# A lead scale per column in the down projection of a fused cross-attention and mixture-of-experts kernel

## Chip, cores and metric

One core of a Trainium2 chip. The metric is device time in microseconds, the median of three runs; a profiled execution was taken beside them.

## What is computed

```python
x = x + jnp.tanh(g_xattn[0]) * _L0_xattn_ref(ctx_512, _layernorm(x, axis=-1), L0_xattn_W, L0_xattn_b)
x = x + jnp.tanh(g_ffn[0]) * _L0_ffn_ref(_layernorm(x, axis=-1), L0_ffn_gate_w, ...)

# _L0_ffn_ref, for all tokens, with E, K, H, I, GS = (16, 4, 512, 384, 128)
probs = jax.nn.softmax(x @ gate_w.T, axis=-1)
vals, idx = jax.lax.top_k(probs, K)
w = vals / jnp.sum(vals, axis=-1, keepdims=True)
combine = jnp.einsum('tke,tk->te', jax.nn.one_hot(idx, E, dtype=x.dtype), w)
w_gu = dequant_fp4(gate_up_packed, gate_up_scales)
act = swiglu(jnp.einsum('th,ehi->eti', x, w_gu))
w_d = dequant_fp4(down_packed, down_scales)
y_e = jnp.einsum('eti,eih->eth', act, w_d)
out = jnp.einsum('te,eth->th', combine, y_e)
act_s = swiglu(x @ dequant_fp4(shared_gate_up_packed, shared_gate_up_scales))
out = out + act_s @ dequant_fp4(shared_down_packed, shared_down_scales)
```

x is 4 x 512 tokens of 512. Every token goes through one shared expert and four of sixteen routed ones. A weight is a 4-bit code times an fp32 scale, one scale per output column and group of 128 input rows; a routed down matrix has three such groups (`IC` = 3).

## The kernel before

**Products.** fp32 accuracy is had from f16 products: an activation is split into a high and a low f16 half, and so is a scale, so that a weight is the sum of two f16 tiles, code times high scale and code times low scale (`wdn[:, buf, hl]`, and `wgu` likewise). For each group three products are summed in PSUM: high x high, high x low, low x high. The down projection of one tile of 128 tokens is therefore nine products of 128x128 by 128x512 (`down`, L1235).

**Tiles and slots.** The shared expert takes sixteen tiles of 128 tokens. Meanwhile the kernel routes: it sorts tokens by expert into slots of up to 128 tokens, 72 slots in all with these inputs. The experts take 4, 5, 5, 4, 4, 4, 5, 5, 4, 5, 4, 4, 4, 5, 5 and 5 slots. Each engine runs its own program over the slots.

- TensorE (`slot`): first half of gate/up, transposes of the last slot's activation (L1221), transposes of the next slot's rows (L1247), second half of gate/up (L1207), then the down products of the slot before. A down group waits for `yev_done`, the evacuation of y two slots earlier (two PSUM banks, `y_ps`).
- ScalarE: `sg` (silu, L615), the high half of `act` (L622), two copies out of PSUM (L629, L640), and `take_y`, which copies y to SBUF with a constant scale (L646).
- VectorE: `act` (L991), the low half (`low_halves`, L996), and the dequant of the *next* expert's weights. `dequant` has four gate/up parts and four down parts (L897 to L933) and `expert` lays them out by hand, one pair beside each slot: in the first slot after `act` part 0 of down and part 1 of gate/up, in the next two likewise; then the copy of the following expert's words (`take_words`, L945), the last down part beside the fourth slot and the first gate/up part for the expert after. `dqg_ready` (L950) and `dq_ready` (L956) tell TensorE that the weights are there.
- GpSimd: for slot s it gathers the rows of slot s + 4, copies slot s's row numbers (`idx_s`, L520), waits for y (`yev_done`) and issues the scatter that adds y to the output in DRAM (L530).
- SP issues the loads and stores. `load_words` brings an expert's codes, `load_scales` its scale halves, both counted on the semaphore `ld_w[buf]`, for which `take_words` waits: 9 loads an expert, 16 counts each.

**The front.** All scales are loaded as one block and split by five VectorE operations (L709 to L713); SP stores the halves to DRAM, from where `load_scales` spreads them over partitions for each expert. Then come layer norm, the cross-attention mix (`attend`, L755), the dequant of the shared expert, and the first two shared tiles' `act`. Behind the last down part of the shared expert VectorE copies expert 1's words (`take_words(1, 1)`), then adds the mix for batch 1 (`attend(1)`), adds the first y (`add_y`, L1000) and takes the statistics of batch 1.

**Order.** Every engine's order is the order of the code; nothing reorders. A wait holds all behind it on its engine.

## Time and profile before

| | |
|---|---|
| median of 3 runs | 688.45 us (687.16 to 690.41) |
| the profiled execution | 687.41 us, its span 685.6 us, mean granted TensorE clock 0.982 of 2.4 GHz |
| busy in the span | PE 629.7 us (92%), DVE 488.1 (71%), ACT 325.3 (47%), POOL 326.2 (48%) |
| instructions | 17258; L1207 x2112 and L1235 x792 on TensorE |
| DMA | 93.72 MB, mean 137 GB/s |

PE is TensorE, DVE VectorE, ACT ScalarE, POOL GpSimd, SPq the queue of SP. "Busy" is a mean over stages: up to about 180 us the shared expert and the routing run, from 184 to 675 us the routed slots. The time of one execution is its span and 1.8 us around it.

### The profile page before, as it was taken

Reading aid. Unit: us, or ns where it says so; the run is one execution under the profiler, and the core shown is the slowest. Engines: PE = TensorE matmul, PEld = TensorE weight load, DVE = VectorE, ACT = ScalarE, POOL = GpSimd, SP = SyncE. Lnnn points to the kernel's source line nnn. Section 1 sums busy time; section 2 is a strip of 40 time slices with the busy share of each in tenths; the row PEclk is TensorE's granted clock in tenths of the full one; section 3 lists DMA queues with packets and bytes.
Section 4 is the critical chain, followed back from the end, with each engine's and each line's share of the span. In section 5 each row is a group of like instructions: output and inputs, shape, how many; then the busy total and the mean of one; then the engine's idle time right before and its main releaser. Section 6 shows DMA issues by size and latency. Waiting matters only on the chain.

```text
span 685.6 us, 17258 instructions
## 1 busy us (share of the span) xinstructions
PE 629.7 (92%) x4394; PEld 382.1 (56%) x4395; DVE 488.1 (71%) x1271; ACT 325.3 (47%) x558; POOL 326.2 (48%) x506
## 2 busy tenths in 40 slices
PE   3768969999998999999999999999999999999992
PEld 2444536557554656565665656566565656656561
DVE  6979779895766858588888767778588878767110
ACT  1763567331343455454544554454554545455541
POOL 3621834100334465564646555464655656565432
PEclk9999989999999999999999999999999999999997
DMA  8780101128157875768587594847767587654533
GB/s 234 202 247 2 63 31 64 62 54 276 49 172 160 189 173 127 176 123 195 110 203 176 126 223 74 226 85 201 168 135 183 117 199 158 152 86 77 93 39 39
DMA packets 49841, 93.72 MB, mean 137 GB/s; under 512 B 8840, under 2 KB 16776, under 8 KB 49816
## 3 DMA queue, kind: packets, MB, share of 16 engines
q0 software_dynamic: 16128, 38.35, 30.3%
q1 hardware_dynamic: 32936, 55.04, 27.5%
q8 instruction: 11, 0.18, 0.1%
q10 hardware_dynamic: 752, 0.04, 0.1%
q14 instruction: 14, 0.11, 0.0%
HBM read 65.16 MB, written 28.24 MB: 136 GB/s over the span
## 4 chain that ended last, share of the span: by engine, by line
PE 80%; DVE 6%; DMA 3%; ACT 3%; POOL 3%; issue 2%; SPq 1%; DVEq 0%; POOLq 0%; ACTq 0%
PE gu_ps L1207 45%; PE bank L1235 22%; PE bank L1247 4%; PE bank L1221 4%; DMA dn_sc<-dn_scale_halves 2%; PE bank L1262 1%; DMA room_a<-in_ctx 1%; PE gu_ps L1167 1%; POOL room_a L462 1%; PE bank L1164 1%; PE bank L1191 1%; DVE stats L725 1%; POOL X L445 1%; DVE X L1000 1%; ACT mix_room L581 1%
## 5 line engine op out<-in xcount | busy, mean ns | idle before, releaser
L1207 PE MATMUL gu_ps<-wgu,mix_room 128*128 x1728 | 305.9, 327 | 2.7 <-DVE tick L950 1.6
L1207 PEld LDWEIGHTS gu_ps<-wgu,mix_room 128*128 128x128 f16 x1728 | 166.5, 98 | 114.7 <-issue 7.5
L1235 PE MATMUL bank<-wdn,aT 128*128 (+1 forms) x792 | 186.2, 380 | 3.2 <-ACT aT L629 2.6
L530 POOL DMA_INDIRECT out<-mix_room,idx_s x72 | 122.9, 1707 | 32.4 <-issue 30.9
L629 ACT ACTIVATE aT<-bank 128x768 f16<-128x768 f16 x88 | 71.2, 809 | 139.5 <-PE bank L1221 136.2
L1235 PEld LDWEIGHTS bank<-wdn,aT 128*128 128x128 f16 x792 | 77.6, 98 | 88.8 <-issue 3.6
L501 POOL TENSOR_TENSOR pool_tick<-ones 128x1 f32<-128x1 f32 x144 | 35.7, 248 | 163.6 <-DMA out<-mix_room,idx_s 84.0
L991 DVE SCALAR_TENSOR_TENSOR act<-gu_ps,wslot,sg x72 | 44.5, 618 | 96.4 <-ACT sg L615 84.8
L622 ACT ACTIVATE acth<-act 128x384 f16<-128x384 f32 x88 | 46.0, 523 | 120.1 <-DVE act L991 120.1
L512 POOL DMA_INDIRECT room_b<-token_rows,idx_g x72 | 76.0, 1055 | 12.3 <-issue 3.6
L927 DVE TENSOR_TENSOR wgu<-dq_code,gu_sc 128x768 f16<-128x768 f16 x136 | 72.5, 574 | 2.3
L640 ACT ACTIVATE mix_room<-bank 128x1024 f16<-128x1024 f16 x72 | 73.1, 1015 | 0.0
L1207 PE MATMUL gu_ps<-wgu,xT 128*128 128x384 f16 x384 | 72.7, 344 | 0.0
L615 ACT ACTIVATE sg<-gu_ps 128x384 f32<-128x384 f32 x88 | 43.1, 490 | 61.0 <-PE gu_ps L1207 61.0
L509 POOL COPY idx_g<-room_b 128x1 int32 (+1 forms) x72 | 39.3, 546 | 67.8 <-DVE tick L861 47.2
L996 DVE TENSOR_TENSOR acth<-act,acth (+1 forms) x88 | 49.2, 559 | 29.7 <-ACT acth L622 29.3
L1207 PEld LDWEIGHTS gu_ps<-wgu,xT 128*128 128x128 f16 x384 | 37.8, 102 | 26.2 <-issue 6.0
L1221 PE MATMUL bank<-id,acth 128*128 128x128 f16 x528 | 43.8, 219 | 8.1 <-ACT acth L622 6.0
L1221 PEld LDWEIGHTS bank<-id,acth 128*128 128x128 f16 x528 | 36.1, 98 | 21.8 <-ACT acth L622 10.0
L1247 PE MATMUL bank<-id,room_b 128*128 128x128 f16 x576 | 44.2, 220 | 0.0
L933 DVE TENSOR_TENSOR wdn<-dn_code,dn_sc 128x384 f16<-128x384 f16 x136 | 43.4, 360 | 0.7
L646 ACT ACTIVATE mix_room<-bank 128x512 f32<-128x512 f32 x72 | 41.7, 579 | 3.0 <-PE bank L1235 3.0
(157 smaller groups left out, 588.1 us busy)
## 6 DMA issues: line engine op xcount, KB each, us to landing
dn_sc<-dn_scale_halves SPq DMA_DIRECT2D x34, 384.0 KB
dn_raw<-in_L_ffn_down_packed SPq DMA_DIRECT2D x48, 256.0 KB
gu_sc<-gu_scale_halves SPq DMA_DIRECT2D x34, 192.0 KB
X<-in_x SPq DMA_DIRECT2D x4, 1024.0 KB, 8.4
token_rows<-room_a SPq DMA_DIRECT2D x16, 256.0 KB, 2.2
out<-X SPq DMA_DIRECT2D x4, 1024.0 KB, 11.1
gu_raw<-in_L_ffn_gate_up_packed SPq DMA_DIRECT2D x16, 192.0 KB
gu_raw<-in_L_ffn_gate_up_packed SPq DMA_DIRECT2D x16, 191.9 KB
```

Source lines behind the costliest of these rows:

```text
L512: nc.gpsimd.indirect_dma_start(xg[:, b, :], None, rows_dram[:, :], bass.IndirectOffsetOnAxis(idx_g[:, b:b + 1], 0)).then_inc(xg_ld[b], 16)
L530: nc.gpsimd.indirect_dma_start(out[:, :], bass.IndirectOffsetOnAxis(idx_s[:, b:b + 1], 0), y_sb[:, b, :], None, compute_op=ALU.add).then_i ...
L622: nc.scalar.activation(acth[:, b, 0, :], act[:, b, :], ACT.Copy).then_inc(ah_done, 1)
L629: nc.scalar.activation(aT[:, b].rearrange("p a c t -> p (a c t)"), at_ps, ACT.Copy).then_inc(aT_done, 1)
L640: nc.scalar.activation(xTs[:, b, :], xT_ps, ACT.Copy).then_inc(xTs_done, 1)
L927: link(nc.vector.tensor_tensor(wgu[:, buf, hl, c, :], dq_code[:, :], gu_sc[:, buf, hl, :], ALU.mult), wait=False)
L991: nc.vector.scalar_tensor_tensor(act[:, b, :], gu_ps[:, 2 + b, 0:I], weight, sg[:, b, :], ALU.mult, ALU.mult).then_inc(act_done, 1)
L996: nc.vector.tensor_tensor(acth[:, b, 1, :], act[:, b, :], acth[:, b, 0, :], ALU.subtract).then_inc(al_done, 1)
L1207: mm = nc.tensor.matmul(ps[b][:, 0:I], x(xp * HC + c), wgu[:, w, wp, c, col:col + I], start=(c == 0 and xp == 0 and wp == 0), stop=(c == H ...
L1221: mm = nc.tensor.transpose(at_ps[:, k * P:(k + 1) * P], acth[:, b, hl, t * P:(t + 1) * P], id16[:, :])
L1235: mm = nc.tensor.matmul(y_ps[0 if shared else b][:, :], aT[:, b, ap, t, :], wdn[:, w, wp, t, :], start=(n == 0), stop=(n == 3 * IC - 1))
L1247: mm = nc.tensor.transpose(xT_ps[:, k * P:(k + 1) * P], chunk_h(halves[:, k // HC, :], k % HC), id16[:, :])
```

## The change

The down scales of a routed expert are divided by a *lead* scale per column: that of the first group, so that the first group's scale becomes 1 (where a column's first scale is zero or far smaller than the others, the largest power of two of the others takes its part). A scale of 1 has no low half, so the product high x low of the first group falls away: eight down products per slot. The lead is multiplied back onto y: VectorE takes y out of PSUM times the lead row (`scale_y`), where ScalarE copied it. The shared expert keeps its nine products.

For that
- the routed down scales are loaded apart (`ld_dn`, `dn_all`), the leads found by `lead_exponents` (ahead of the shared dequant) and `lead_scales` (behind its second down part), which also splits the divided scales into halves;
- SP stores those halves and the leads to DRAM when `dn_split` comes, among the stores of token rows, and only then loads expert 1's scales;
- the lead row of each expert is loaded to all partitions (`load_lead`), those of experts 1 and 2 behind the output stores and waited for in `expert(0)` behind `add_y`, the others with the expert's loads;
- `dequant` leaves out the low half of the first group;
- in an expert of five slots or more, the slots from the fourth on all run ahead of the last down part.

```diff
             for b in range(1, B):
                 load_ctx(b)
             load_x(1)
+            for t in range(IC):
+                sp.dma_start(dn_all[:, t, :], dn_scales[:, t, :].rearrange("e (b n) -> e b n", n=HB)).then_inc(ld_dn, 16)
...
             load_words(sp, gu_packed[0], dn_packed[0], 1)
-            sp.wait_ge(st_sc, 64)
-            load_scales(sp, 1, 1)
             for i in range(NT):
+                if i == TB:
+                    sp.wait_ge(dn_split, 1)
+                    for hl in range(2):
+                        for t in range(hl, IC):
+                            sp.dma_start(dn_s_dram[hl, 1:, t, :].rearrange("e (b n) -> e b n", n=HB),
+                                         dn_h[:, hl, t, :]).then_inc(st_dn, 16)
+                    sp.dma_start(lead_dram.rearrange("e (b n) -> (e b) n", n=HB), lead_s[:, :]).then_inc(st_dn, 16)
+                    sp.wait_ge(st_sc, 32)
+                    sp.wait_ge(st_dn, 16 * (2 * IC - 1 + 1))
+                    load_scales(sp, 1, 1)
...
+            for n in (1, 2):
+                load_lead(sp, n, ld_lead)
             sp.wait_ge(dq_ready, 2)
             load_expert(sp, gu_packed[2], dn_packed[2], 1, 3)
+            load_lead(sp, 3, ld_w[1])
...
-            def take_y(r, b):
-                a.wait_ge(y_done, NT + r + 1)
-                if not isinstance(r, int) or r >= 2:
-                    a.wait_ge(added[b], 8 * (r - b))
-                nc.scalar.activation(y_sb[:, b, :], y_ps[b][:, :], ACT.Copy, scale=1.0 / W_SCALE).then_inc(yev_done, 1)
...
                     for hl in range(2):
-                        link(nc.vector.tensor_tensor(wdn[:, buf, hl].rearrange("p t n -> p (t n)")[:, cols],
-                                                     dn_code[:, 0:COLS],
-                                                     dn_sc[:, buf, hl].rearrange("p t n -> p (t n)")[:, cols], ALU.mult),
+                        skip = 0 if hl == 0 or shared else max(0, H - d * COLS)
+                        if skip >= COLS:
+                            continue
+                        part = slice(d * COLS + skip, (d + 1) * COLS)
+                        link(nc.vector.tensor_tensor(wdn[:, buf, hl].rearrange("p t n -> p (t n)")[:, part],
+                                                     dn_code[:, skip:COLS],
+                                                     dn_sc[:, buf, hl].rearrange("p t n -> p (t n)")[:, part], ALU.mult),
...
+                    if d == 1:
+                        lead_scales()
                     activations(d // 2, d // 2, shared_w[:, 0:1])
...
+            def scale_y(r, n):
+                v.wait_ge(y_done, r + NT + 1)
+                v.wait_ge(idx_s_ready, r + 1)
+                nc.vector.tensor_tensor(y_sb[:, r % 2, :], y_pair[:, r % 2, :],
+                                        lead_y[:, bass.ds(n - 1, 1), :].rearrange("p k n -> p (k n)"), ALU.mult).then_inc(yev_done, 1)
...
             def routed_slot(r, e):
                 head(r, e)
                 low_halves(r + NT, r % 2)
+                scale_y(r - 1, e + 1)
...
                 if add_last:
                     add_y(NT - 1)
+                    v.wait_ge(ld_lead, 32)
+                else:
+                    scale_y(first - 1, e)
                 for k in range(1, PARTS - 1):
                     with v.If(tiles > k):
                         head(first + k, e)
                         dequant(n, buf_next, k + 1, k, fill=lambda: low_halves(first + k + NT, (first + k) % 2))
+                        scale_y(first + k - 1, e + 1)
                     with v.Else():
                         dequant(n, buf_next, k + 1, k)
                 end_gate_up(n, buf_next)
                 with v.If(tiles > PARTS - 1):
-                    routed_slot(first + PARTS - 1, e)
+                    with v.Fori(PARTS - 1, tiles) as k:
+                        routed_slot(first + k, e)
                 dequant(n, buf_next, None, PARTS - 1)
                 end_dequant(n)
-                with v.If(tiles > PARTS):
-                    with v.Fori(PARTS, tiles) as k:
-                        routed_slot(first + k, e)
...
+                terms = [(t, ap, wp) for t in range(IC) for ap, wp in ((0, 0), (0, 1), (1, 0))
+                         if shared or t or not wp]
```

The order of SP's queue in the front, before: expert 1's words, its scales right behind, then the sixteen stores of token rows (L379).

```order
L309 DMA gu_raw<-in_L_ffn_gate_up_packed 64x1535
L312 DMA dn_raw<-in_L_ffn_down_packed 128x1x512 x3
L318 DMA gu_sc<-gu_scale_halves 128x1x768 [waits st_sc]
L318 DMA gu_sc<-gu_scale_halves 128x1x768
L321 DMA dn_sc<-dn_scale_halves 128x1536 x2
L379 DMA token_rows<-room_a 128x512 [waits xl_ready,xh_ready] x16
```

The same stretch of SP's queue now:

```order
L336 DMA dn_raw<-in_L_ffn_down_packed 128x1x512 x3
L416 DMA token_rows<-room_a 128x512 [waits xl_ready,xh_ready] x4
L408 DMA dn_scale_halves<-wgu 16x8x64 [waits dn_split]
L408 DMA dn_scale_halves<-wgu 16x8x64 x4
L410 DMA dn_lead_scales<-lead_s 128x64
L342 DMA gu_sc<-gu_scale_halves 128x1x768 [waits st_dn,st_sc]
L342 DMA gu_sc<-gu_scale_halves 128x1x768
L346 DMA dn_sc<-dn_scale_halves 128x1536
L346 DMA dn_sc<-dn_scale_halves 128x1024
L416 DMA token_rows<-room_a 128x512 [waits xl_ready,xh_ready] x12
```

The four loads of scales moved behind four row stores, six new stores and a wait for `dn_split`.

VectorE in the third slot of a routed expert, before, from the unpacking of the codes to the copy of the next words:

```order
L916 TENSOR_SCALAR dn_bits<-dn_bits 128x384
L919 TENSOR_SCALAR dq_code<-dq_mag 128x768 [waits dequant_step]
L922 TENSOR_SCALAR dn_code<-dn_bits 128x384
L927 TENSOR_TENSOR wgu<-dq_code,gu_sc 128x768 [waits dequant_step]
L927 TENSOR_TENSOR wgu<-dq_code,gu_sc 128x768
L933 TENSOR_TENSOR wdn<-dn_code,dn_sc 128x384 x2
L1121 UNCONDITIONAL_BRANCH
```

And the same place now, with the branch around it:

```order
L985 TENSOR_SCALAR dn_bits<-dn_bits 128x384
L988 TENSOR_SCALAR dq_code<-dq_mag 128x768 [waits dequant_step]
L991 TENSOR_SCALAR dn_code<-dn_bits 128x384
L996 TENSOR_TENSOR wgu<-dq_code,gu_sc 128x768 [waits dequant_step]
L996 TENSOR_TENSOR wgu<-dq_code,gu_sc 128x768
L1006 TENSOR_TENSOR wdn<-dn_code,dn_sc 128x384 x2
L1175 REGISTER_ALU
L1177 ISA [waits idx_s_ready,y_done]
L1177 REGISTER_ALU
L1177 TENSOR_TENSOR mix_room<-y_pair,xT 128x512
L1210 UNCONDITIONAL_BRANCH
```

The multiply of the last slot's y (`mix_room` holds `y_sb`, `xT` the lead rows) stands behind the dequant part, with a wait for GpSimd (`idx_s_ready`) and TensorE (`y_done`). In the fourth slot it stands right behind the low half (L1070):

```order
L1065 SCALAR_TENSOR_TENSOR act<-gu_ps,wslot,sg 128x384
L1070 ISA [waits ah_done]
L1070 TENSOR_TENSOR acth<-act,acth 128x384
L1175 REGISTER_ALU
L1177 ISA [waits idx_s_ready,y_done]
L1177 ISA
L1177 TENSOR_TENSOR mix_room<-y_pair,xT 128x512
L1218 REGISTER_ALU
L1218 COMPARE_AND_BRANCH
```

Before, the low half was followed there by the branch and the last down part; the multiply is new between them.

## Rows read from the trace of the kernel before

**Rows 1.** The page, part 4: the chain that ended last, by engine.
```profile
PE 80%; DVE 6%; DMA 3%; ACT 3%; POOL 3%; issue 2%; SPq 1%; DVEq 0%; POOLq 0%; ACTq 0%
```

**Rows 2.** The chain in order of time, one routed slot: start us, us, what.
```profile
413.20 1.95 PE gu_ps L1207 x12
415.15 1.94 PE bank L1235 x9
...
419.83 1.30 PE gu_ps L1207 x8
```

**Rows 3.** VectorE's timeline, one expert: start us, us, instruction, [idle before <-releaser].
```profile
309.24 0.62 DVE L991 SCALAR_TENSOR_TENSOR act<-gu_ps,wslot,sg  x1 [0.20 <-issue]
310.59 0.56 DVE L996 TENSOR_TENSOR acth<-act,acth  x1 [0.74 <-ACT acth L622]
...
316.89 0.62 DVE L991 SCALAR_TENSOR_TENSOR act<-gu_ps,wslot,sg  x1 [1.01 <-issue]
...
321.86 0.67 DVE L933 TENSOR_TENSOR wdn<-dn_code,dn_sc 128x384 f16<-128x384 f16 x2
322.84 0.62 DVE L991 SCALAR_TENSOR_TENSOR act<-gu_ps,wslot,sg  x1 [0.31 <-issue]
...
329.55 0.62 DVE L991 SCALAR_TENSOR_TENSOR act<-gu_ps,wslot,sg  x1 [1.34 <-ACT sg L615]
...
336.12 0.62 DVE L991 SCALAR_TENSOR_TENSOR act<-gu_ps,wslot,sg  x1 [0.30 <-issue]
```

**Rows 4.** VectorE's timeline in the front.
```profile
28.63 0.56 DVE L945 COPY gu_half<-gu_raw 128x768 uint16<-128x768 uint16 x1 [1.04 <-DMA dn_sc<-dn_scale_halves]
...
50.78 0.62 DVE L991 SCALAR_TENSOR_TENSOR act<-gu_ps,shared_w,sg 128x384 f32<-128x384 f32 x1 [3.48 <-ACT sg L615]
```

**Rows 5.** The chain in order of time, in the front.
```profile
57.84 0.08 DVE gu_half L945
...
58.31 2.73 DVE X L755 x4
```

**Rows 6.** VectorE's timeline while routing: small operations.
```profile
144.34 0.20 DVE L817 CAST pos_slot<-pos_i 128x64 f16<-128x64 int32 x1
...
147.37 0.42 DVE L791 TENSOR_REDUCE r_sum<-r_exp 128x16 f32<-128x256 f32 x1
```

**Rows 7.** SP's timeline in the front, and by tile the landing of the scale stores.
```profile
18.46 1.25 SPq L318 DMA_DIRECT2D gu_sc<-gu_scale_halves  x2
...
DMA to landing us min/median/max: 4.0/5.0/6.0
```

**Rows 8.** Timelines of VectorE and GpSimd, first routed expert.
```profile
196.18 0.62 DVE L991 SCALAR_TENSOR_TENSOR act<-gu_ps,wslot,sg  x1 [0.62 <-ACT sg L615]
...
201.48 0.18 POOL L520 COPY idx_s<-room_b 128x1 int32<-128x1 int32 x1 [5.59 <-DMA out<-X]
...
214.45 0.57 DVE L945 COPY gu_half<-gu_raw 128x768 uint16<-128x768 uint16 x1 [4.15 <-DMA dn_sc<-dn_scale_halves]
```

**Rows 9.** VectorE's timeline: first `act` of the second and of the last routed expert.
```profile
222.79 0.62 DVE L991 SCALAR_TENSOR_TENSOR act<-gu_ps,wslot,sg  x1 [0.96 <-ACT sg L615]
...
642.90 0.62 DVE L991 SCALAR_TENSOR_TENSOR act<-gu_ps,wslot,sg  x1 [4.65 <-ACT sg L615]
```

**Rows 10.** VectorE's timeline: the add of y to X and the instruction behind it.
```profile
60.96 0.68 DVE L1000 SCALAR_TENSOR_TENSOR X<-bank,X 128x512 f32<-128x512 f32 x1
61.56 0.68 DVE L725 BATCH_NORM_STATS2 stats<-X 128x6 f32<-128x512 f32 x1
```

**Rows 11.** Timelines of ScalarE and GpSimd: y evacuated, scatter, next index copy.
```profile
397.48 0.58 ACT L646 ACTIVATE mix_room<-bank 128x512 f32<-128x512 f32 x1
...
398.90 1.61 POOL L530 DMA_INDIRECT out<-mix_room,idx_s  x1 [0.50 <-issue]
...
413.36 1.61 POOL L530 DMA_INDIRECT out<-mix_room,idx_s  x1 [0.15 <-issue]
...
416.64 0.19 POOL L520 COPY idx_s<-room_b 128x1 int32 x1
```

More of the change, by code:

```diff
@@ L213, in gated_xattn_moe @@
         gu_ps = psum("gu_ps", [P, 4, 512], F32)
-        bank = [gu_ps[:, i, :] for i in range(4)] + [psum(f"bank{i}", [P, 512], F32)[:, :] for i in range(4, 8)]
+        bank4 = psum("bank4", [P, 512], F32)
+        y_pair = psum("y_pair", [P, 2, 512], F32)
+        bank7 = psum("bank7", [P, 512], F32)
+        bank = [gu_ps[:, i, :] for i in range(4)] + [bank4[:, :], y_pair[:, 0, :], y_pair[:, 1, :], bank7[:, :]]
         g_ps, u_ps = bank[0:2], bank[2:4]
@@ L719, in _, with lead_exponents @@
                                          ALU.logical_shift_left), wait=False)
+            s0, s1, s2 = (dn_all[:, t, :] for t in range(IC))
+            e_rest, e_lead, reach, keep, up, own, other, inv = (lead_room[:, k, :] for k in range(8))
+            def lead_exponents():
+                EXPONENT, TINY, DEEP = 0x7F800000, 2.0 ** -100, 2.0 ** -20
+                v.wait_ge(ld_dn, 16 * IC)
+                step(nc.vector.tensor_scalar(e_rest.bitcast(I32), s1.bitcast(I32), EXPONENT, None, ALU.bitwise_and), wait=False)
+                step(nc.vector.tensor_scalar(up.bitcast(I32), s2.bitcast(I32), EXPONENT, None, ALU.bitwise_and), wait=False)
+                step(nc.vector.tensor_scalar(e_lead.bitcast(I32), s0.bitcast(I32), EXPONENT, None, ALU.bitwise_and))
+                step(nc.vector.scalar_tensor_tensor(e_rest, e_rest, TINY, up, ALU.max, ALU.max))
+                step(nc.vector.scalar_tensor_tensor(keep, e_rest, DEEP, e_lead, ALU.mult, ALU.is_le), wait=False)
+                step(nc.vector.scalar_tensor_tensor(reach, e_rest, DEEP, e_lead, ALU.mult, ALU.max))
@@ L867, in _ @@
             G_STEPS, D_STEPS = 6, 5
[L868 removed]
+            N_STEPS = PARTS * (G_STEPS + D_STEPS)
             def end_of(n):
[L872 removed]
+                return (n + 1) * N_STEPS + (1 if isinstance(n, int) and n == E else 2)
             def dequant(n, buf, g, d, fill=None, free=None):
[L878 removed]
+                shared = isinstance(n, int) and n == 0
+                if shared:
                     done = 1 + g * G_STEPS if d is None else 1 + PARTS * G_STEPS + d * D_STEPS
                 elif d is None:
[L881 removed]
+                    done = n * N_STEPS + 2
                 elif g is None:
@@ L979, in _ @@
             row_scores(3)
+            lead_exponents()
             take_words(0, 0)
@@ L1109, in expert @@
                 if buf_next is None:
-                    routed_slot(first, e)
+                    head(first, e)
+                    low_halves(first + NT, first % 2)
+                    scale_y(first - 1, e)
                     with v.If(tiles > 1):
```

83 lines of the change are left out of this document (59 added, 24 removed).

## The prediction

> **What bounds the kernel now.** I read the chain that ended last first. TensorE holds 80% of it and VectorE 6% [rows 1]. In order of time, one routed slot is two gate/up halves of 1.95 us, some transposes, and nine down products in 1.94 us; it comes round every 6.63 us [rows 2]. So TensorE sets the pace, and one product out of nine is 0.216 us. Seventy-two slots make 15.6 us, if nothing else is close.
>
> Something is close. I went through VectorE's timeline over one expert with four slots [rows 3], because VectorE dequantizes the next expert's weights during this expert's slots and must be done by their end. The starts of its `act` instruction lie 7.65, 5.95, 6.71 and 6.57 us apart. Where the idle time before `act` is put down to ScalarE's `sg`, VectorE waited for data; where it says "issue", VectorE itself was late. Only the third distance holds such a wait (1.34 us), so VectorE's own time there is 5.37 us. Its four slots take 7.65 + 5.95 + 5.37 + 6.57 = 25.5 us, TensorE's 4 x 6.63 = 26.5 us. VectorE has 1.0 us to spare in an expert of four slots, and there are eight such experts; the other eight have five.
>
> In the front the chain runs through VectorE itself: the copy of expert 1's words (L945) at 57.84, then `attend`, the statistics and GpSimd [rows 4, 5]. A wait there is on the path one for one.
>
> **The change, part by part.** The sum is made on the profiled execution, 687.4 us, which is 1.0 us under the median of the runs; I add that at the end.
>
> *Scales in the front.* Today expert 1's scales are stored and loaded before VectorE needs them. Now they exist only after `lead_scales`, 15 dependent operations put behind the second down part of the shared expert. VectorE idles there from 47.30 (50.78 less 3.48) [rows 4]. A 64-wide operation took 0.20 us, a 256-wide one 0.42, some 0.04 between them [rows 6]; nine of the first and six of the second kind at 192 wide, some 0.35, are 4.2 us (bounds 3.0 and 6.9). Of these 3.5 lie in the idle time. The halves are ready at 51.5. SP then issues six stores, by the two issues in its row at some 0.6 us each, and a store of scales lands 4.0 to 6.0 us after its issue, median 5.0 [rows 7]; the sixth, issued 3 us after the first, is there at about 59. Only then do the four loads of scales start. For the shared expert the same four were issued from 18.46 and VectorE was released at 28.63 [rows 4, 7], 10.2 us; I take 10, since the queue is emptier and one load a third smaller. That is 69, against 57.84. VectorE's program waits for all loads of that buffer in front of `attend`, so add_y, the statistics and all that follow stand still: **+11 us** (bounds 7 and 15.5: 3.0, 2.5, 4.0 and 8 us, or 6.9, 3, 6.0 and 10.2, counted from 47.3). SP has nothing else to do then; the next row stores wait for the same chain.
>
> The six operations of `lead_exponents` lie where VectorE waits for shared scales anyway (1.04 us before 28.63 [rows 4]); nothing. If they push the start by a microsecond, TensorE's first gate/up, which the chain puts behind transposes, still hides it. The first split is narrower; nothing.
>
> *First expert.* VectorE now waits for the lead rows of experts 1 and 2 behind its last `add_y`. SP issues them behind the last output tile. GpSimd saw that tile landed at 201.48, after 5.59 us of waiting [rows 8]; half that many bytes more take some 2 us, so 203.4. VectorE's `act` of the second slot was at 196.18. Its three remaining slots of this expert, at the costs below (6.1, 7.2, 9.4), end at 226.1 if nothing holds them, 226.8 with a little of TensorE's delay, where the next expert began at 222.79 [rows 9]. The 4.15 us it waited at 214.45 for the next weights [rows 8] vanish, since it comes later itself. **+4 us** (bounds 1 and 6).
>
> *Fourteen experts with a dequant beside them.* Before, from 222.79 to 642.90, 420.1 us [rows 9]. TensorE alone would now need 6.63 - 0.216 = 6.41 a slot: 25.7 and 32.1 us for four and five slots, 404.6 in all. VectorE gets one multiply per slot, 512 wide from PSUM and SBUF. The nearest row is the add to X of the same shape out of the same bank: 0.68 us long, the next instruction starting 0.60 after it [rows 10]. I take 0.62, with its register work hidden behind the running operation. It loses the low half of the first group's down part (half of 0.67 [rows 3]) and a third of a multiply in the second. The Trainium skill ("VectorE: DVE Perf Modes", the section on the TRN2 errata) gives (N+151)/0.96, 691 ns, for an fp32 tensor_tensor; by it the sum would be about 4 us higher. The trace, in which the next instruction starts before the record ends, decides.
>
> A second cost is a new handshake. The multiply waits until GpSimd has copied that slot's index, which lies behind the scatter of the slot before. From ScalarE's copy (ended 398.06) to the scatter's issue it took 0.84 us, from an issue (413.36) to the end of the next index copy 3.47 [rows 11]; together 4.3. In the first three slots VectorE comes to its multiply after the dequant part, about 6 us after the last. In the fourth it comes right behind `low_halves`, about 2.9 us after: 1.0 for the copy of words and 1.9 from `act` to the end of the low halves [rows 3]. So it waits 1.4 us. Four slots then cost 5.95 + 0.62 - 0.33 - 0.1 = 6.1; 5.37 + 0.2 + 0.62 - 0.1 = 6.1; 6.57 + 0.62 = 7.2; 7.4 + 0.62 + 1.4 = 9.4 (7.65 has the loop's back edge, which every second expert has, so 7.4): 28.8 us, over TensorE's 25.7. In five slots the fourth has no dequant: 1.9 + 1.4 + 0.62 + 0.3 = 4.2; the last 7.4 + 0.62 + 1.0 = 9.0. That is 32.6, plus some 1.0 in which VectorE stands waiting for TensorE in the short slot: 33.6. Seven of each are 436.8 us: **+16.7**, the 15.6 us of products already taken out.
>
> Bounds. Below: a multiply of 0.5 and no wait for GpSimd, 26.9 and 32.2 us, 414 in all, -6. Above: 0.25 us of register work per slot and waits of 2.2, 30.6 and 36, 466 in all, +46. ScalarE loses a copy of 0.58 us per slot [rows 11]; it waits elsewhere, so nothing. The extra lead load of each expert comes three slots before it is needed; nothing.
>
> *The last expert* has no dequant: five slots at TensorE's pace, **-1 us**; in the tail VectorE takes y in place of ScalarE, nothing.
>
> Sum: 687.4 + 11 + 4 + 16.7 - 1 = 718.1; on the runs' scale **719 us**.
>
> **Rivals.**
> - *VectorE keeps up.* TensorE still bounds the slots; the fourteen experts fall to 404.6 us (-15.5), the first expert costs +1, the front +11: 684 us, faster. For it: VectorE is far from full on the average over all slots. Against it: the four-slot sum of 25.5 us has no room for four multiplies; it decides when the sum stays under 25.7. With the front hidden as well it would be 674. Chance 0.08 for the two.
> - *The multiply is cheap.* At a third of ScalarE's 0.58 us it is 0.2; the sums fall to 27.1 and 32.6, 418 in all (-2), first expert +3: 699 us. The add to X speaks against it [rows 10]. The Trainium skill ("ScalarE: Activation LUTs", Rules for kernel authors) sends multiplies to VectorE, as up to three times faster in bf16; this one reads fp32 from PSUM. Chance 0.07.
> - *The front is hidden.* If the scales land before VectorE asks, or other work fills the wait: +1 for +11, 709 us. Against it: copy and `attend` are neighbours on the chain [rows 5]. Chance 0.08.
> - *The handshake rules.* Waits for GpSimd or register work in most slots, experts of 30 and 35 us, 455 in all (+35), front and first expert as above: 738 us. Chance 0.15.
>
> **How the numbers follow.** The forecast has 0.62 and by itself runs from 708 to 729. A measurement tells 0.5% from no change, 3.4 us, so same is 685.0 to 691.9. The first rival is mostly under that: faster 0.07; the edges of the first two give same 0.05; slower 0.88. Leaving out the fast end and the upper tail of the handshake, the range is 697 to 741.
>
> **What would show it.** Right: VectorE idle some 10 us before the copy of expert 1's words, released by a load of scales; some 7 us behind the last add_y, released by a lead row; TensorE waiting for ScalarE's or VectorE's act in each expert, most in its last slot; nine products gone to eight at 1.73 us; VectorE over 90% busy from the second expert to the fourteenth. Wrong: slots evenly 6.4 us apart, `act` still behind `sg` everywhere, or the copy of words at its old time.

## The result, and the profile after

The changed kernel takes 758.1 us in the median of four runs (754.04 to 760.26) against 688.7: a ratio of 1.10, interval 1.0947 to 1.1054. The forecast was 719, its range 697 to 741; the sign was right, and the loss is twice and more what was forecast. The profiled execution has a span of 755.9 us, 70.3 more than before.

The page of the changed kernel, busy time by engine, and the chain that ended last:

```profile
PE 636.9 (84%) x4322; PEld 381.0 (50%) x4323; DVE 524.3 (69%) x1314; ACT 290.2 (38%) x486; POOL 332.7 (44%) x506
...
PE 32%; DVE 24%; issue 15%; DMA 10%; POOL 8%; DVEq 5%; ACT 4%; SPq 1%; POOLq 1%; ACTq 0%
```

TensorE's share of the chain falls from 80% [rows 1] to 32%. Its busy time is 7.2 us longer than before, though 72 products of 0.216 us are gone. VectorE, which was to be the bound, is busy 69% of the span, no more than before (71%). So no engine is full; the engines stand waiting for each other. The forecast had given "VectorE over 90% busy from the second expert to the fourteenth" as a sign of being right; it is 72% from 225 to 450 us (162.31 of 225, in the stretches below).

VectorE's timeline at the ends of the stages: the copy of expert 1's words, then the first `act` of the first routed expert, the second `act`, and the first `act` of the second and of the last expert.

```profile
67.78 0.56 DVE L1018 COPY gu_half<-gu_raw 128x768 uint16<-128x768 uint16 x1 [6.57 <-DMA dn_sc<-dn_scale_halves]
...
198.91 0.62 DVE L1065 SCALAR_TENSOR_TENSOR act<-gu_ps,wslot,sg  x1 [0.90 <-ACT sg L658]
...
214.12 0.62 DVE L1065 SCALAR_TENSOR_TENSOR act<-gu_ps,wslot,sg  x1 [9.50 <-DMA xT<-dn_lead_scales]
...
239.36 0.62 DVE L1065 SCALAR_TENSOR_TENSOR act<-gu_ps,wslot,sg  x1 [0.86 <-issue]
...
714.38 0.62 DVE L1065 SCALAR_TENSOR_TENSOR act<-gu_ps,wslot,sg  x1 [1.31 <-issue]
```

Against [rows 4, 8, 9] and the first routed `act` of before (189.59 us), the stages give:

| step | forecast | measured |
|---|---|---|
| front, to the first routed `act` | +11 | +9.3 |
| first expert | +4 | 40.4 for 33.2: +7.2 |
| fourteen experts | +16.7 | 475.0 for 420.1: +54.9 |
| last expert and tail | -1 | 41.5 for 42.7: -1.2 |

So 38 of the 39.6 us that the sum is short of lie in one step. There an expert takes 31.4 us with four slots and 36.5 with five (forecast 28.8 and 33.6; before 27.1 and 32.9). From VectorE's timeline, the last slots of an expert of four, then (from 344.12) the first slot of the next:

```profile
332.30 0.69 DVE L1177 TENSOR_TENSOR mix_room<-y_pair,xT  x1 [0.50 <-POOL idx_s L563]
...
333.87 0.62 DVE L1065 SCALAR_TENSOR_TENSOR act<-gu_ps,wslot,sg  x1 [0.39 <-issue]
335.23 0.56 DVE L1070 TENSOR_TENSOR acth<-act,acth  x1 [0.74 <-ACT acth L665]
337.87 0.69 DVE L1177 TENSOR_TENSOR mix_room<-y_pair,xT  x1 [2.09 <-POOL idx_s L563]
338.48 0.41 DVE L979 TENSOR_SCALAR dn_bits<-dn_raw,dn_shift 128x384 int32<-128x384 int32 x1
...
344.12 0.62 DVE L1065 SCALAR_TENSOR_TENSOR act<-gu_ps,wslot,sg  x1 [0.97 <-issue]
...
352.68 0.62 DVE L1065 SCALAR_TENSOR_TENSOR act<-gu_ps,wslot,sg  x1 [2.84 <-ACT sg L658]
```

and TensorE's in the same time:

```profile
340.34 2.11 PE L1295 MATMUL gu_ps<-wgu,mix_room 128*128 x12
346.15 0.80 PE L1309 MATMUL bank<-id,acth 128*128 128x128 f16 x6 [3.69 <-ACT acth L665]
346.74 1.06 PE L1336 MATMUL bank<-id,room_b 128*128 128x128 f16 x8
347.59 4.05 PE L1295 MATMUL gu_ps<-wgu,mix_room 128*128 x12
```

and GpSimd's, the scatter of the slot before, the next gather with its index, and the index for which VectorE waits:

```profile
333.83 1.61 POOL L573 DMA_INDIRECT out<-mix_room,idx_s  x1 [0.30 <-issue]
334.89 0.92 POOL L552 COPY idx_g<-room_b 128x1 int32 x1
335.90 0.19 POOL L544 TENSOR_TENSOR pool_tick<-ones 128x1 f32<-128x1 f32 x1
336.23 1.02 POOL L555 DMA_INDIRECT room_b<-token_rows,idx_g  x1
337.26 0.19 POOL L563 COPY idx_s<-room_b 128x1 int32 x1
```

In the expert's last slot (act at 333.87) VectorE waits 2.09 us for the index, multiplies, and has the last down part and the next gate/up part still to do: the next `act` comes 10.25 us later. TensorE stands still 3.69 us for it. Then it runs slower: the same twelve products take 4.05 us that took 2.11 before the stop. So the `act` behind comes another 8.56 us later, and now it is VectorE that waits (2.84 us for ScalarE's `sg`, which waits for TensorE). Both kinds of wait in the groups of waits, from 239.4 to 714.4 us, that is, over the fourteen experts (us in total, times, longest):

```profile
DVE mix_room L1177 <- POOL idx_s L563: 46.8, 24, 3.2
DVE act L1065 <- ACT sg L658: 37.7, 28, 2.9
...
PE bank L1309 <- ACT acth L665: 47.6, 14, 4.7
```

The stretches view of the changed kernel (stretch, its length, busy time and count of PE, PEld, DVE, ACT and POOL, then the granted clock of TensorE, DMA share and GB/s):

```profile
225.00:450.00 225.00, 201.17 (x1364) 119.56 (x1362) 162.31 (x396) 84.31 (x148) 114.32 (x175) 0.95 0.66 144
...
346.00:352.00 6.00, 5.85 (x29) 3.58 (x30) 3.73 (x10) 2.20 (x4) 1.51 (x3) 0.53 1.05 258
352.00:358.00 6.00, 6.00 (x46) 3.74 (x45) 5.01 (x14) 2.52 (x5) 1.91 (x5) 1.00 0.66 159
```

and of the kernel before:

```profile
223.00:440.00 217.00, 216.25 (x1537) 130.59 (x1536) 161.76 (x402) 108.15 (x196) 122.21 (x194) 1.00 0.72 163
```

The clock falls from 1.00 to 0.95 over the experts; in the six microseconds behind the stop it is 0.53 of 2.4 GHz, near its lower level of 1.2 GHz, and 1.00 again after.

Not every stop is followed by this. Behind ten of the fourteen (2.71 to 4.67 us long) the twelve products take 3.26 to 4.05 us; behind the other four (2.70 to 3.08 us) they take 2.11, as here:

```profile
315.50 0.49 PE L1309 MATMUL bank<-id,acth 128*128 128x128 f16 x6 [2.95 <-ACT acth L665]
...
316.28 2.11 PE L1295 MATMUL gu_ps<-wgu,mix_room 128*128 x12
```

The ranges overlap, so the length of a stop alone does not decide it. The three experts of four slots begun at full pace took 30.6, 31.3 and 31.1 us, the four begun with slow products 32.2, 31.1, 31.0 and 32.4: the clock makes some 0.7 us of the 2.6 by which such an expert exceeds the forecast.

### The profile page after: what moved, and what is told of

It is laid out like the page before. It is cut to its first block, busy times and chain, and to the rows that moved or that the text cites. A ratio compares the mean times of both kernels' runs of the same rounds, so it can differ in the third digit from the quotient of the medians.

```text
span 755.9 us, 17257 instructions
## 1 busy us (share of the span) xinstructions
PE 636.9 (84%) x4322; PEld 381.0 (50%) x4323; DVE 524.3 (69%) x1314; ACT 290.2 (38%) x486; POOL 332.7 (44%) x506
## 3 DMA queue, kind: packets, MB, share of 16 engines
q0 software_dynamic: 16128, 38.35, 28.8%
## 4 chain that ended last, share of the span: by engine, by line
PE 32%; DVE 24%; issue 15%; DMA 10%; POOL 8%; DVEq 5%; ACT 4%; SPq 1%; POOLq 1%; ACTq 0%
PE gu_ps L1295 19%; PE y_pair L1324 7%; DMA out<-mix_room,idx_s 4%; DVE act L1065 3%; DVE wgu L996 2%; POOL room_b L555 2%; DMA dn_sc<-dn_scale_halves 2%; PE bank L1309 2%; ACT acth L665 2%; DVE mix_room L1177 2%; DVE dn_bits L979 2%; PE bank L1336 2%; DVE wdn L1006 2%; DVE dn_code L991 2%; DVE dn_bits L985 2%
## 5 line engine op out<-in xcount | busy, mean ns | idle before, releaser
L1295 PE MATMUL gu_ps<-wgu,mix_room 128*128 x1728 | 322.6, 339 | 4.3 <-DVE tick L1023 3.4
L1295 PEld LDWEIGHTS gu_ps<-wgu,mix_room 128*128 128x128 f16 x1728 | 171.8, 101 | 126.0 <-issue 26.2
L1324 PE MATMUL y_pair<-wdn,aT 128*128 (+1 forms) x720 | 174.4, 387 | 9.1 <-DVE X L1074 4.5
L544 POOL TENSOR_TENSOR pool_tick<-ones 128x1 f32<-128x1 f32 x144 | 38.2, 266 | 224.4 <-DVE mix_room L1177 157.7
L573 POOL DMA_INDIRECT out<-mix_room,idx_s x72 | 119.1, 1654 | 31.7 <-issue 31.4
L1324 PEld LDWEIGHTS y_pair<-wdn,aT 128*128 128x128 f16 x720 | 71.6, 100 | 90.4 <-issue 14.7
L552 POOL COPY idx_g<-room_b 128x1 int32 (+1 forms) x72 | 61.3, 851 | 64.0 <-DVE tick L929 46.6
L1177 DVE TENSOR_TENSOR mix_room<-y_pair,xT (+1 forms) x72 | 49.5, 688 | 52.5 <-POOL idx_s L563 49.0
L555 POOL DMA_INDIRECT room_b<-token_rows,idx_g x72 | 80.0, 1111 | 10.8 <-issue 0.9
L1070 DVE TENSOR_TENSOR acth<-act,acth (+1 forms) x88 | 49.2, 559 | 29.7 <-ACT acth L665 29.6
L1295 PEld LDWEIGHTS gu_ps<-wgu,xT 128*128 128x128 f16 x384 | 38.5, 104 | 32.7 <-issue 13.2
L982 DVE TENSOR_TENSOR dq_mag<-dq_mag,dq_sign 128x768 uint16<-128x768 uint16 x68 | 39.0, 573 | 2.3
```

Source lines behind the costliest of these rows:

```text
L552: nc.gpsimd.tensor_copy(idx_g[:, b:b + 1], tok[:, bass.ds(s, 1)]).then_inc(idx_g_ready, 1)
L555: nc.gpsimd.indirect_dma_start(xg[:, b, :], None, rows_dram[:, :], bass.IndirectOffsetOnAxis(idx_g[:, b:b + 1], 0)).then_inc(xg_ld[b], 16)
L573: nc.gpsimd.indirect_dma_start(out[:, :], bass.IndirectOffsetOnAxis(idx_s[:, b:b + 1], 0), y_sb[:, b, :], None, compute_op=ALU.add).then_i ...
L1177: nc.vector.tensor_tensor(y_sb[:, r % 2, :], y_pair[:, r % 2, :], lead_y[:, bass.ds(n - 1, 1), :].rearrange("p k n -> p (k n)"), ALU.mult) ...
L1295: mm = nc.tensor.matmul(ps[b][:, 0:I], x(xp * HC + c), wgu[:, w, wp, c, col:col + I], start=(c == 0 and xp == 0 and wp == 0), stop=(c == H ...
L1324: mm = nc.tensor.matmul(y_ps[0 if shared else b][:, :], aT[:, b, ap, t, :], wdn[:, w, wp, t, :], start=(n == 0), stop=(n == len(terms) - 1))
```

## The experiments

**Theory** after the result: the wait for the index and the multiply make VectorE late once in each expert; TensorE stops, and the stop is not made up. **Rivals**: VectorE's work as such is the bound; the order of the loops is; the waits in the front and for the leads return elsewhere.

**1. The index a slot ahead** (GpSimd).

```diff
-                    pool.wait_ge(added[b], 8 * (s - b))
-                nc.gpsimd.tensor_copy(idx_s[:, b:b + 1], tok[:, bass.ds(s, 1)]).then_inc(idx_s_ready, 1)
...
+                    pool.wait_ge(added[1 - b], 8 * (s + b))
+                nc.gpsimd.tensor_copy(idx_s[:, 1 - b:2 - b], tok[:, bass.ds(s if last else s + 1, 1)]).then_inc(idx_s_ready, 1)
                 pool.wait_ge(yev_done, s + 1)
```

> The changed kernel, but GpSimd copies the row numbers of slot s+1 before it waits for y of slot s (as soon as the scatter of slot s-1 has landed), so that the multiply no longer stands behind a scatter and a gather. In the changed kernel VectorE lost 49.0 us to that index in 25 waits of about 2 us, mostly in the last slot of an expert, where TensorE then stood still for 3.7 to 4.7 us and its first gate/up half after the stop took 3.1 to 4.1 us in place of 1.95. Theory 'handshake': the waits go, the last slot's distance falls from 10.2 to about 8.1 us, TensorE's stop is halved and part of the clock comes back: 14 experts times 2 to 3 us, so 715 to 730 us. Rival 'VectorE's work': the multiply and the parts of the dequant that the last slot now carries set the pace, and the wait only fills what would be lost anyway: at most 8 us less, 750 or more.

725.3 us, 1.054 (1.0507 to 1.0581): 32.8 us less, as the handshake theory had it. The fourteen experts fall to 444.0 us, the granted clock from 225 to 660 us is 0.99. From the waits of this run from 240 to 680 us, VectorE's, TensorE's and GpSimd's:

```profile
DVE mix_room L1174 <- POOL idx_s L566: 2.6, 4, 0.9
...
PE bank L1333 <- DMA room_b<-token_rows,idx_g: 13.7, 14, 2.0
...
POOL pool_tick L565 <- DMA out<-mix_room,idx_s: 140.6, 63, 6.2
```

VectorE's wait is gone, and others stand in its place: GpSimd waits longer for the scatter before (140.6 us; in the changed kernel 56.9 from 225 to 680), and TensorE for rows gathered too late.

**2. ScalarE copies y, twice tried.** `scale_y` and its calls are taken out of VectorE's program, `take_y` is put back into ScalarE's; the lead scale is left out of the result.

> The changed kernel, but ScalarE copies y out of PSUM with the constant scale, as before, and VectorE neither multiplies nor waits for the index; the lead scale per column is left out of the result. Eight products, the front, the lead loads and the new order of the loops stay. Theory 'all of it is VectorE's multiply and its wait': the fourteen experts fall from 475.0 us to TensorE's pace, 404.6 to 412, and the total is 687 to 696 us (the front's +9.3 and the first expert's +7.3 remain). Rival 'the order of the loops': the last down part and the first gate/up part in the last slot stop TensorE also without the multiply; then the fourteen experts stay above 430 and the total above 712.

747.8 us, 1.087 (1.084 to 1.0891). By the total that is the rival's, but not by the slots: four experts of five slots took 32.1 to 32.7 us, near TensorE's pace, beside others with one slot of 11 to 13 us. TensorE's waits from 240 to 680 us and the packets of instructions (page, part 3) of this run:

```profile
PE bank L1305 <- issue: 46.1, 12, 10.0
...
q14 instruction: 39, 0.32, 0.2%
```

Shorter code had moved VectorE's loop. So the run was repeated with padding ahead of it:

```diff
-        LEAD = 30
+        LEAD = 68
```

> The run in which ScalarE copies y again, with 68 memsets in place of 30 at the head of VectorE's program, so that VectorE's loop over pairs of experts lies again where it lay in the kernel before (instructions 688 to 987, there 688 to 1013). In the run with 30 VectorE and TensorE stood still up to 10 us at the loop's head for nothing that the trace names but 'issue', and 39 packets of instructions were loaded where the changed kernel loads 15. The lead scale is left out of the result again. Theory 'code loading hid the answer, and VectorE's multiply with its wait is the whole loss': the stops at the loop's head go, packets of instructions fall back to 14 or 15, the fourteen experts take 405 to 415 us and the total is 688 to 698. Rival 'the order of the loops': the experts of four slots stay above 29 us without any stop at the loop's head, total above 705.

694.1 us, 1.0075 (1.0049 to 1.01), 14 such packets, and the fourteen experts at 416.7 us (27.0 and 32.5). The same kernel, 38 memsets longer, is 53.6 us faster. So VectorE's multiply with its wait is worth 475.0 - 416.7 = 58.3 us in the experts, more than the 54.9 that they lost. The order of the loops by itself costs little: experts of five slots, the only ones whose order changed, take 32.5 us here and 31.9 in the old order with the same eight products (experiment 3). (To put back the old order with the multiply in place was not tried: VectorE's loop would grow, and the code's place would speak into the result again. What the order does to the multiply's wait stays open.)

**3. Eight products alone**, in the kernel before.

```diff
-                for t in range(IC):
-                    for ap, wp in ((0, 0), (0, 1), (1, 0)):
+                terms = [(t, ap, wp) for t in range(IC) for ap, wp in ((0, 0), (0, 1), (1, 0))
+                         if shared or t or not wp]
```

> The kernel before with eight down products per routed slot: the product high x low of the first group is left out, nothing else is changed (the result loses that small part). It prices the saving by itself. Theory 'TensorE sets the pace and VectorE just keeps up' (25.5 us of VectorE's work against 25.7 of TensorE's in an expert of four slots): 72 x 0.216 = 15.5 us less, 673 us. Rival 'VectorE is already the bound where the expert has four slots': these eight experts gain nothing and the others 1.08 each, so 679 to 681 us.

680.3 us, 0.9895 (0.9864 to 0.9927). The rival was right: of 15.5 us, some 8.5 come through. Experts of five slots gain 1.0 us (32.9 to 31.9), those of four 0.2 (27.1 to 26.9): VectorE already held them.

**4. Front and leads.** `take_words(1, 1)` moves to the fifth shared tile, the first two lead rows ahead of expert 2's loads.

```diff
-            take_words(1, 1)
             attend(1)
...
                 if i == 5:
+                    take_words(1, 1)
                     first_weights(0)
...
+            for n in (1, 2):
+                load_lead(sp, n, ld_lead)
             sp.wait_ge(dq_ready, 1)
...
-            for n in (1, 2):
-                load_lead(sp, n, ld_lead)
             sp.wait_ge(dq_ready, 2)
```

> The changed kernel with two moves: the copy of expert 1's words, which waits for expert 1's scales, is put right before the first use of those words (behind the fifth shared tile), and the lead rows of experts 1 and 2 are loaded before expert 1's successor is loaded, not behind the output stores. Theory 'both waits are on the path one for one': the idle time of 6.57 us before the copy of the words and of 9.50 us before the act of the second routed slot go; act of the first routed slot comes at 192 to 193 in place of 198.9 (the 3.3 us of lead_scales stay), the first expert takes 33 to 35 us in place of 40.45; 743 to 747 us in all. Rival 'other work fills them': the waits reappear later (in the shared tiles, or at the next expert's weights) and the total stays above 753.

743.8 us, 1.080 (1.0764 to 1.0844). The first routed `act` comes at 192.6, the first expert takes 34.3 us, the fourteen stay at 474.0: both waits were on the path. A wait of 4.7 us for the next expert's loads comes back in the first expert, where the kernel before had 4.15 [rows 8]. With experiment 1:

> The index copied a slot ahead and the two moves of front and leads together. If the three waits lie one behind the other on the path and have nothing to do with each other, the savings add: 725.3 less 14.4 = 711 us, within 3. If one hides another, the total stays above 716.

714.4 us, 1.037 (1.0332 to 1.041): 11.0 of the 14.4 us add, between what was expected for "add" (711, within 3) and for "hide" (over 716).

**5. The index before the gather**, with front and leads.

```diff
+                    index(2 * j + b - 2, b)
                     gather(2 * j + b + 2, b)
                     add(2 * j + b - 2, b)
```

(`index` holds the wait for `added[b]` and the copy that stood at the head of `add`.)

> The changed kernel with the two moves of front and leads, and with GpSimd copying the index of slot s right behind the scatter of slot s-1, before the gather of slot s+4 and not behind it. No scatter waits for more than it does in the changed kernel. In the run that copied the index a whole slot ahead every scatter waited for the one before, GpSimd stood 140.6 us for that from 240 to 680 us, and TensorE waited 13.7 us for rows gathered too late. Theory 'those 13.7 us were the price of the remedy, not of the multiply': the wait for the index stays away, TensorE waits for no rows, the fourteen experts take 425 to 435 us in place of 443.7, and the total falls from 714.4 to 696 to 706. Rival 'VectorE's own work is what is left': the fourteen experts stay at 440 or more, 711 us or more.

706.4 us, 1.025 (1.0225 to 1.0274), just past the edge of what the first theory gave (696 to 706, the experts 425 to 435). TensorE waits 0.5 us for rows in place of 13.7, VectorE 9.3 us for the index from 225 to 640 us, and the fourteen experts take 436.2. Of the 58.3 us, then, some 38 hang on the handshake (474.0 to 436.2), 19 on the multiply and what is left of its wait (436.2 to 416.7), and 1 came with the moves of experiment 4.

**6. GpSimd multiplies**, in SBUF, after ScalarE's copy.

```diff
+                e = pool.value_load(slot_i[0:1, bass.ds(s, 1)], min_val=0, max_val=E - 1)
                 pool.wait_ge(yev_done, s + 1)
...
+                nc.gpsimd.tensor_tensor(y_sb[:, b, :], y_sb[:, b, :], lead_y[:, bass.ds(e, 1), :].rearrange("p k n -> p (k n)"),
+                                        ALU.mult).then_inc(scaled, 1)
+                pool.wait_ge(scaled, s + 1)
```

> ScalarE copies y out of PSUM as before, and GpSimd, which has to wait for y anyway before it issues the scatter, multiplies it by the lead row in SBUF; nothing else waits for the index. The two moves of front and leads are in it, lead_scales runs beside the third shared tile, and VectorE's program has 68 memsets at its head, so that its loop lies where it did. Theory 'VectorE had no room for the multiply, GpSimd has': act of the first routed slot at 190 to 193 us, the first expert 33 to 35 us, the fourteen experts 405 to 414 (VectorE's own work still sets the experts of four slots, as in the kernel before with eight products), total 673 to 684 us, faster than before. Rival 'GpSimd is too slow or slows VectorE': a multiply of 128x512 on GpSimd beyond 2 us makes scatter and gather late, or VectorE's instructions beside it grow; then the fourteen experts stay above 420 and the total above 690.

766.5 us, 1.111 (1.1069 to 1.1144): the rival's total, but not by its condition, a multiply beyond 2 us: it took 1.27, and the rest of GpSimd's round made the rows late. A second version has one register load less:

> GpSimd multiplies again, with less around it. In the first of these runs the multiply itself took 1.27 us, but GpSimd's round was 7.1 to 8 us a slot, in which two loads of a register took 1.36, and TensorE waited 24.9 us for gathered rows. Now one load is gone (the scatter waits for the scatter before it in every slot, behind the multiply), and lead_scales is back behind the second down part. Theory 'GpSimd's round was the bound': it falls to about 6.4 us, the fourteen experts to 416 to 430, the total to 683 to 697. Rival 'GpSimd can't carry the multiply in any such order': the round stays above 7 us, the total above 710.

735.0 us, 1.066 (1.0632 to 1.0692): less loss, and the rival's total again, though the round is as short as the theory had it. GpSimd's timeline in that run:

```profile
370.68 0.19 POOL L568 TENSOR_TENSOR pool_tick<-ones 128x1 f32<-128x1 f32 x1 [0.73 <-POOL idx_s L564]
370.82 1.27 POOL L569 TENSOR_TENSOR mix_room<-mix_room,xT 128x512 f32<-128x512 f32 x1
...
372.51 1.63 POOL L575 DMA_INDIRECT out<-mix_room,idx_s  x1 [0.15 <-issue]
373.56 0.78 POOL L553 COPY idx_g<-room_b 128x1 int32 x1
...
374.88 1.04 POOL L556 DMA_INDIRECT room_b<-token_rows,idx_g  x1
...
377.05 0.46 POOL L568 TENSOR_TENSOR pool_tick<-ones 128x1 f32<-128x1 f32 x1 [0.73 <-POOL idx_s L564]
```

Its round is 6.4 us (370.68 to 377.05) where it waits for nobody, as long as TensorE's slot, so there is no room in it for the waits for a landed scatter, 40.9 us in all from 225 to 640, and TensorE waits 27.4 us for rows. That the one makes the other is read from these rows; no run takes the waits away.

**7. Work for TensorE in the stop.** Fifteen fp32 products between the gate/up half and the transposes, in the slot behind an expert's first.

```diff
                 gate_up(s, b, x, w, 0)
+                if not isinstance(r, int):
+                    e_1 = pe.value_load(slot_i[0:1, bass.ds(r - 1, 1)], min_val=0, max_val=E - 1)
+                    e_2 = pe.value_load(slot_i[0:1, bass.ds(r - 2, 1)], min_val=0, max_val=E - 1)
+                    with pe.If(e_1 > e_2):
+                        for _ in range(15):
+                            nc.tensor.matmul(bank4[:, IC * P:], id32[:, :], id32[:, :], start=True, stop=True)
```

> The changed kernel, with 15 fp32 products of 128x128 by 128x128 put into TensorE's program at the place where it stands still for VectorE's act in each expert after the second (between the first gate/up half and the transposes, only in the slot behind an expert's first); their output is never read. They add work and take no wait away. In the changed kernel the gate/up half behind such a stop takes 3.1 to 4.1 us in place of 1.95, and the clock granted from 225 to 450 us is 0.95 against 1.00 before. Theory 'the stop costs twice, once as a wait and once through the clock': behind the filler the gate/up half takes 1.95 to 2.3 us, the distance behind the late act falls from 7.6 or 8.5 to 6.0 to 6.6, and the total falls by 12 to 22 us, to 736 to 746. Rival 'the slow products come from something else, or VectorE's own work fills that time anyway': total 755 or more.

774.9 us, 1.125 (1.1211 to 1.1285). The first half of the theory holds: the granted clock from 225 to 640 us is 1.00, and behind the filler the gate/up half takes 2.11 us, so the slow products come with the stop.

```profile
345.06 3.61 PE L1419 MATMUL bank<-id 128*128 128x128 f32 x30 [0.41 <-issue]
...
349.29 2.11 PE L1295 MATMUL gu_ps<-wgu,mix_room 128*128 x12
```

What that is worth in time it does not tell: the two register loads and the branch stand in every slot (TensorE idle "issue" before the transposes 16.3 us, 34 times), second slots that took 6.5 us now take up to 7.3, and the products outlast the wait. Experiments 8 and 9 ask the question from the other side.

**8, 9. A stop alone.** The padded run of experiment 2 (66 memsets in place of 68), with one useless reduction on VectorE in an expert's last slot.

```diff
+                nc.vector.tensor_reduce(extra[:, :], X[:, 0:5, :], mybir.AxisListType.XY, ALU.add)
                 dequant(n, buf_next, None, PARTS - 1)
```

> The run in which ScalarE copies y (694.1 us; lead scale left out), and VectorE gets one useless reduction of 128x2560 elements per expert, some 2.7 us, at the place where the changed kernel multiplies and waits for the index in an expert's last slot; it reads X and its output is never read. Nothing is added in the other slots. If VectorE's sum over an expert against TensorE's is what counts, as in the prediction's sum, these 2.7 us mostly fall into VectorE's idle time: the fourteen experts rise from 416.7 to 430 at most, the total to 706 at most. Theory 'a stop of TensorE is never made up': it costs its own length and the slow clock behind it, the slot behind the stop takes 7.4 us or more where it took 6.0, the fourteen experts rise to 455 to 470, and the total to 730 to 748 with a granted clock of 0.94 to 0.96 from 225 us on.

The reduction takes 2.81 us. 746.8 us, 1.085 (1.0817 to 1.0878), as the theory of the stop had it; the fourteen experts rise by 48.8 us to 465.5 (30.5 and 36.1), 3.5 us for each 2.81, and TensorE's busy time from 618.9 to 638.6 for the same 4322 instructions. In eleven of the fourteen the slot behind the late `act` takes 7.2 us or more, in eight of them the 7.4 that was expected.

```diff
-                nc.vector.tensor_reduce(extra[:, :], X[:, 0:5, :], mybir.AxisListType.XY, ALU.add)
+                nc.vector.tensor_reduce(extra[:, :], X[:, 0:5, 0:H // 2], mybir.AxisListType.XY, ALU.add)
```

> The same as the run with the useless reduction in an expert's last slot, with half as many elements (128x1280): some 1.4 us in place of 2.81. The 2.81 us cost 48.8 us in the fourteen experts, 3.5 each, and TensorE's busy time rose from 618.9 to 638.6 us for the same 4322 instructions. Theory 'a long stop also takes the clock, a short one does not': TensorE's busy time stays under 624 us, the fourteen experts rise by no more than the added work, to 430 to 437 us, the total is 706 to 715. Rival 'every microsecond of a stop costs the same': half of 48.8, so 441 us for the fourteen experts, TensorE's busy time near 629, 718 to 722 in all.

The reduction takes 1.48 us. 717.9 us, 1.042 (1.0393 to 1.0445); the fourteen experts 437.9 us, 1.5 us more for each 1.48, TensorE busy 627.2 us. It falls between the two, nearer to the rival (718 us, 441, 629). The price is not quite even, though: the first 1.48 us cost 21.2 us in all, the next 1.33 us 27.6. TensorE's timeline around a stop in this run, and around one with the longer reduction:

```profile
330.73 2.11 PE L1293 MATMUL gu_ps<-wgu,mix_room 128*128 x12
335.07 0.49 PE L1307 MATMUL bank<-id,acth 128*128 128x128 f16 x6 [2.22 <-ACT acth L666]
...
335.85 2.11 PE L1293 MATMUL gu_ps<-wgu,mix_room 128*128 x12
```

```profile
336.23 2.12 PE L1293 MATMUL gu_ps<-wgu,mix_room 128*128 x12
341.80 0.80 PE L1307 MATMUL bank<-id,acth 128*128 128x128 f16 x6 [3.45 <-ACT acth L666]
342.40 1.06 PE L1334 MATMUL bank<-id,room_b 128*128 128x128 f16 x8
343.25 2.74 PE L1293 MATMUL gu_ps<-wgu,mix_room 128*128 x12
```

Behind the stop of 2.22 us TensorE goes on at its pace; behind that of 3.45 us the transposes take 0.80 us in place of 0.49. In the shorter run only three of the fourteen slots behind a stop take 7.5 us or more (their stops are 2.21 to 2.28 us long, and others of 2.22 and 2.23 kept the pace), in the longer one eleven take 7.2 or more.

Each run so holds both cases, and expert by expert against the padded run they part the price. Where the products behind the stop kept their pace, 1.48 us cost 1.14 on the mean of eleven experts and 2.81 us cost 2.43 on the mean of three; where they were slow, 2.89 (three) and 3.77 (eleven). So most of a stop is never made up even at the full clock, and the low clock adds some 1.3 to 1.8 us to an expert of these runs.

## Why the prediction missed

**Right.** *Front:* VectorE was released by a load of scales at 67.78 (forecast 69), the fifteen operations took 4.6 us (4.2; the terms as written there sum to 4.5). That the sum came so near was in part luck. VectorE reached these operations at 49.59 and not at 47.30, since the shared scales had released it 2.2 us later than before (30.80 against 28.63), which the sum did not have; and the stores of the new scales landed 1.8 us after their issue and not 5.0. *The last expert.* *The mechanism of the experts:* the wait for GpSimd's index falls in the last slot, and the multiply costs VectorE 0.61 us from start to start (337.87 to 338.48; forecast 0.62). The record itself is 0.686 us. The Trainium skill ("VectorE: DVE Perf Modes", the section on the TRN2 errata) gives 0.691 for it, which agrees with the record and not with what the engine is held.

**Wrong, the step that failed:** "Fourteen experts with a dequant beside them", in it the sentence that ends "28.8 us, over TensorE's 25.7". An expert was priced at the larger of two sums, VectorE's and TensorE's, as if work late in one slot were made up in the next. For the most part it is not: where the sum had 28.8 us for VectorE and 25.7 for TensorE, an expert took 31.4, because each engine stopped the other in turn, TensorE in the last slot (47.6 us in the fourteen experts), VectorE for ScalarE's `sg` behind it. Of that last wait the sum had 7 us (1.0 in each expert of five slots); the runs show 37.7. Experiments 8 and 9 show it bare: in a kernel whose experts had VectorE waiting for `sg` 52.5 us from 225 to 640, 2.81 us put into one slot cost 3.5 an expert and 1.48 us cost 1.5, and still 2.4 and 1.1 where the clock did not fall.

On top comes the clock, of which the prediction said nothing: behind ten of the fourteen stops the same products take up to 4.05 us in place of 2.11, and TensorE is busy 636.9 us where the kernel before with the same eight products needs 614.8. The Trainium skill ("TensorE: Matmul & The Clock Gate", "HAM oscillation") tells of a kernel whose TensorE waits in every round and so begins every round at the low clock. The granted clock of 0.53 behind the stop at 346 us agrees, and so do nine more of the fourteen rounds; four began at full pace.

Two terms were also mis-sized. *The handshake*: forecast 1.4 us in an expert of four slots and 2.4 in one of five, 26.6 in the fourteen; measured 46.8. A wait is 2.0 long (46.8/24), and VectorE has more of them than one in each expert. VectorE's own work was 12.7 us less than priced, so that the waits for the index (20.2 over) and for `sg` (30.7 over) come to the 38.2 us that the step is short of. From y evacuated to the next index in GpSimd it is 4.5 us (332.99 to 337.45), forecast 4.3, and the way through the semaphore (0.4 us, 337.45 to 337.87) was left out. *The first expert*: the lead rows released VectorE 15.2 us after the first routed `act`; by the sum it was 13.8 (203.4 less 189.6), and the three slots after it took 25.2 us, not 22.7; the +7.2 lies outside the bounds of 1 and 6.

**The rivals.** "The handshake rules" (738 us, experts of 30 and 35 us) was nearest, but the waits did not fall in most slots: 24 in the 63 of the fourteen experts, mostly in those where no dequant part stands before the multiply. "VectorE keeps up" and "the multiply is cheap" fell with the 0.61 us; "the front is hidden" with experiment 4.

No version here that multiplies by the lead scale beats the kernel before. Without wait and multiply the experts reach 416.7 us against 420.1, and front and first expert take back more than that; the moves of experiment 4 were not tried together with it. Moving the multiply of an expert's last slot into the next expert's first was not tried.

## What to carry to other kernels

Two engines that handed each slot on to each other ran here nearly at the pace of the later one in *each* slot, not at the larger of their sums: look for the one slot of a round that is already full, and keep new work and new waits out of it. Before a wait is attached to an event, follow what else stands before that event on its engine; here the index behind the scatter and the gather cost some 38 us, more than twice the 15.6 that the products were worth on paper. A product saved on TensorE was worth only what the other engines' slots left open: 8.5 us (experiment 3).

## What the runs showed that was not expected

- **The place of code.** The same VectorE loop, begun 38 instructions later, made a run 53.6 us faster (747.8 to 694.1). The only marks are "issue" waits at the loop's head (up to 10.0 us on TensorE) and 39 packets of instructions where the others have 14 or 15. Whoever takes instructions out of a loop compares these packets first.
- **GpSimd's register loads.** Each `value_load` costs GpSimd some 0.6 us, half as much as its multiply of 128x512 (1.27): from the copy of the index to the next operation it is 0.16 us idle with none between them (experiment 1), 0.73 with one (the row above) and 1.36 with two (experiment 6).
- **The clock behind a stop**, with the numbers above: 2.11 us of products become 2.74 behind a stop of 3.45 us and 4.05 behind one of 3.69, but stay 2.11 behind one of 2.95.
